# Merged second-layer weights built by GpSimd during levels 2 and 3; image 0: statistics and normalisation ahead of the output and identity products

## The chip, the core and the metric

One core of one Trainium2 chip runs the whole program. The metric is device time in microseconds (us), from start to end of one execution; lower is better. Names of engines in the rows: PE is TensorE (PEld its weight loads), DVE is VectorE, ACT is ScalarE, POOL is GpSimd, SP is SyncE, which here only issues transfers (SPq).

## What is computed

Two residual convolution layers on eight images of 64 channels, 128 by 128. Cut to what matters here:

```python
# layer 0: group norm, then four resolutions (levels 0 to 3) of conv3x3 -> relu -> conv1x1 -> attention
for i in range(LEVELS):                       # level i works at 128 / 2**i
    y = mean_pool(gn(x), 2 ** i)
    y = relu(conv3x3_dilated(y, ds_w3[i])); y = conv1x1(y, ds_w1[i])
    out += upsample(att(y))                   # 13x13 filter plus a dynamic 3x3 filter per image
x = x + conv1x1(out, fin_w)
# layer 1: a 5x5 convolution, and a 3x3 convolution seen through nine shifts weighted by wr
y3, y5 = conv3x3(gn(x)) + b3, conv5x5(gn(x)) + b5
out = einsum(stack([y5] + nine_shifts(y3)), wr) + br
x = x + out
```

In layer 1 both convolutions and the weights `wr` fold into one 5x5 convolution, the *merged weights*, plus corrections for the image borders (`row_w`, `col_w`, `cor_w`). In layer 0 the 1x1 convolutions fold into output products (`gti`, `gar`) and identity weights (`idt_h`, `idt_l`).

## The kernel before

The program is one sequence of blocks: level 1 for all eight images, then levels 2 and 3 together for four pairs of images, then level 0, then layer 1. A block ends when all engines have reached its end; the next one starts then. Every engine runs its own queue in the order of the code, and only semaphores tie the queues. Products of full precision are made as three matmuls, high by high, high by low and low by high (`product`, lines 169 to 171), so most data exist as a high and a low half, for instance `nh`, `nl` (normalised input), `rh`, `rl` (after the relu), `lk_h`, `lk_l` (large filter).

**Level 1, one image after another.** GpSimd sums 2x2 pixels of each chunk of the input (`prep_chunk`, lines 308 to 314) and VectorE takes statistics of the same chunk (line 878). VectorE combines them (line 885), TensorE averages over groups (`group_mean_pe` line 228, `group_var_pe` line 233), VectorE finishes mean and deviation and normalises in five pieces (`norm`, line 906); ScalarE makes `nh` of each piece (line 753), GpSimd `nl` (line 631). TensorE convolves five chunks of rows (`conv`), ScalarE applies the relu (lines 775, 777), VectorE makes `rh` (line 968), GpSimd `rl` (line 687). After `features` and `identity` follows `large_filter`, 28 tiles of three matmuls, of which the last six need this image's dynamic tiles from VectorE. Work for image i+1 (chunks 2 to 7, statistics, normalisation) stands between the steps of image i.

**Image 0** has extra steps. ScalarE issues all small loads before it computes anything. TensorE starts with the output products (lines 1150, 1151), VectorE copies them out (1053, 1054), TensorE makes the identity products (1155 to 1160), and only then come the group means. GpSimd clears `lks` (line 732, before `norm_low`) and SyncE then fills it and issues all other weight loads (`weights`, lines 529 to 536) before it may load chunks 2 and 3 of image 1 into `room`, for which it also waits until the identity weights have left `room` (`s_cp` of 9). GpSimd makes the low half of the large filter (`filter_low`, line 598) after chunks 5 to 7 of image 1.

**Image 7** has the merged weights. GpSimd clears four tiles (`conv5_clear`), ScalarE loads the weights into them, and after its `rl` pieces GpSimd runs `conv5_first` and nine times `conv5_shift` (lines 654 to 676), in tiles that borrow room from level 1 (`pl1`, `pln`, `xc`, `room`). ScalarE copies the result to `tile5` and `col_w` (lines 835, 837), and SyncE stores it to memory (line 592), where layer 1 reads it much later. SyncE's first wait in the next block is for that store.

**Levels 2 and 3, per pair.** GpSimd makes `rl` (line 1330), sums for the next pair, clears columns of the feature tiles (lines 1343, 1344) and makes `nl` of the next pair (line 1323). VectorE makes four sets of dynamic tiles per pair (`dynamic_tiles`, lines 191 to 206, of 768 columns; I call them tiles 1 to 4), the third in `lk_h`, `lk_l`, the others in `dt_h`, `dt_l`. TensorE runs the fixed taps, then the convolutions of the next pair with the dynamic taps in between, in the order of the four tiles. Tile 4 takes the buffer of tile 1 and waits for `dt_f`. After the last pair there are no convolutions to interleave.

## Time and profile before

| what | us |
|---|---|
| median of 3 runs | 2747.36 |
| lowest, highest | 2738.88, 2752.03 |
| the profiled execution | 2754.88 |
| its span, first to last instruction | 2753.1 |
| TensorE busy | 2481.8 (90%) |
| VectorE, ScalarE, GpSimd busy | 2094.9, 1104.4, 943.6 |
| level 1 (image 0 to the store of image 7) | 0 to about 494 |
| merged weights and their store behind it | to 511.7 |
| levels 2 and 3 | 512 to about 821 |

TensorE is busy 90% of the span, so the first question at any place is whether TensorE waits there. A row of the timeline gives start, duration, engine, line, operation, result and source, and in brackets how long the engine had been idle and what released it. "x8" means that neighbouring instructions of one line are merged. Times are from the span's start.

### The profile page before, as it was taken

The numbers are of one execution on the slowest core, as the hardware profiler recorded it, in microseconds if no ns is written. First come the engines' busy times: TensorE is split into PE (matmuls) and PEld (weight loads), VectorE is DVE, ScalarE is ACT, GpSimd is POOL, SyncE is SP. The second block draws the span as 40 slices with busy tenths as digits, with TensorE's granted clock in tenths as the row PEclk, the third lists the DMA queues.
The fourth block names the chain that finished last, engine by engine and source line by source line (L and its number), as shares of the span: only waits on it lengthen the run. The fifth ranks groups of instructions, "written<-read, shape, count | busy, mean of one in ns | idle before, by whom it ended". The sixth has DMA issues, their size and how long they took to land. (4 is left out here: it accounts for less than half of the span.)

```text
span 2753.1 us, 37560 instructions
## 1 busy us (share of the span) xinstructions
PE 2481.8 (90%) x11638; PEld 1990.3 (72%) x11638; DVE 2094.9 (76%) x2776; ACT 1104.4 (40%) x1773; POOL 943.6 (34%) x863
## 2 busy tenths in 40 slices
PE   3899999499978999999995988999849999999998
PEld 3677777388866888888884767777637777777776
DVE  5566564245548888888887898898869899998998
ACT  1332332101107898989993222222113333333331
POOL 6775666522204444444446734444010000000000
PEclk9899999788868999999997988999859999999999
DMA  7344441100008777777762134443442333333332
GB/s 137 88 113 104 102 102 42 35 14 11 10 21 199 221 219 216 222 217 213 221 192 105 65 148 150 156 156 140 166 167 67 111 114 98 96 97 110 116 99 62
DMA packets 345087, 338.82 MB, mean 123 GB/s; under 512 B 57648, under 2 KB 308400, under 8 KB 331696
## 3 DMA queue, kind: packets, MB, share of 16 engines
q1 hardware_dynamic: 337056, 335.53, 41.9%
q10 hardware_dynamic: 7952, 2.30, 0.5%
q8 instruction: 42, 0.69, 0.1%
q14 instruction: 37, 0.30, 0.0%
HBM read 211.60 MB, written 122.62 MB: 121 GB/s over the span
## 5 line engine op out<-in xcount | busy, mean ns | idle before, releaser
L169 PE MATMUL ps_all<-vh,u_h 128*128 128x512 f32 x960 | 384.6, 401 | 29.2 <-DVE vl L2945 28.4
L171 PE MATMUL ps_all<-vh,u_l 128*128 128x512 f32 x960 | 383.0, 399 | 0.0
L170 PE MATMUL ps_all<-vl,u_h 128*128 128x512 f32 x960 | 382.6, 399 | 0.0
L2854 ACT ACTIVATE vh<-rt,gn 128x528 fp32r<-128x528 f32 x192 | 131.0, 728 | 445.2 <-DVE rt L2922 319.4
L169 PE MATMUL ps_all<-vh,t_h 128*128 128x512 f32 x576 | 231.4, 402 | 23.5 <-DVE vl L1984 23.4
L1823 POOL TENSOR_TENSOR zr<-zr,z 128x256 f32<-128x256 f32 x128 | 126.5, 1008 | 336.7 <-DMA xr<-in_x 336.7
L169 PEld LDWEIGHTS ps_all<-vh,u_h 128*128 128x128 f32 x960 | 180.7, 188 | 82.8 <-issue 36.5
L170 PE MATMUL ps_all<-vl,t_h 128*128 128x512 f32 x576 | 230.2, 400 | 0.0
L171 PE MATMUL ps_all<-vh,t_l 128*128 128x512 f32 x576 | 229.4, 398 | 0.0
L171 PEld LDWEIGHTS ps_all<-vh,u_l 128*128 128x128 f32 x960 | 180.9, 188 | 46.2
L170 PEld LDWEIGHTS ps_all<-vl,u_h 128*128 128x128 f32 x960 | 181.0, 189 | 45.4
L169 PE MATMUL ps_all<-nh,w3h 128*128 128x512 f32 (+2 forms) x348 | 135.6, 390 | 45.7 <-POOL nl L1323 35.8
L1827 POOL TENSOR_TENSOR xr<-xr,zr 128x1024 f32<-128x1024 f32 x64 | 146.7, 2292 | 5.0
L169 PEld LDWEIGHTS ps_all<-vh,t_h 128*128 128x128 f32 x576 | 109.2, 189 | 50.4 <-issue 25.0
L1912 ACT ACTIVATE rp_h<-yt,b3p 128x1024 fp32r<-128x1024 f32 x64 | 142.8, 2231 | 0.0
L169 PE MATMUL ps_all<-ch,w_h 128*128 128x512 f32 x280 | 116.2, 415 | 27.0 <-POOL cl L2294 12.8
L2500 DVE TENSOR_TENSOR xq<-xq,ps_all 128x512 f32<-128x512 f32 x128 | 129.5, 1088 | 11.2 <-PE ps_all L2671 9.9
L2294 POOL TENSOR_TENSOR cl<-rw,ch 128x560 fp32r<-128x560 f32 x48 | 80.8, 1686 | 151.0 <-ACT ch L2338 151.0
L170 PE MATMUL ps_all<-nl,w3h 128*128 128x512 f32 (+2 forms) x348 | 131.5, 378 | 0.0
L171 PE MATMUL ps_all<-nh,w3l 128*128 128x512 f32 (+2 forms) x348 | 131.5, 378 | 0.0
L2945 DVE SCALAR_TENSOR_TENSOR vl<-rt,gn,vh 128x1056 fp32r<-128x1056 f32 x96 | 127.2, 1325 | 3.0 <-ACT vh L2854 3.0
L171 PEld LDWEIGHTS ps_all<-vh,t_l 128*128 128x128 f32 x576 | 108.9, 189 | 27.7
(410 smaller groups left out, 6668.4 us busy)
## 6 DMA issues: line engine op xcount, KB each, us to landing
xr<-in_x SPq DMA_DIRECT2D x128, 256.0 KB, 3.6
x_layer<-xr SPq DMA_DIRECT2D x64, 512.0 KB, 2.7
xq<-x_layer SPq DMA_DIRECT2D x32, 1024.0 KB, 4.8
x_layer<-xq SPq DMA_DIRECT2D x32, 1024.0 KB, 3.8
out<-ot SPq DMA_DIRECT2D x64, 512.0 KB, 5.1
xw<-in_x SPq DMA_DIRECT2D x112, 288.0 KB, 4.3
xw<-x_layer SPq DMA_DIRECT2D x16, 1152.0 KB, 8.6
xw<-x_layer SPq DMA_DIRECT2D x16, 1088.0 KB, 7.7
```

The lines of the kernel that those rows point to most:

```text
L169: pe.matmul(o, wh, xh, start=first, stop=False, skip_group_check=True)
L170: pe.matmul(o, wh, xl, start=False, stop=False, skip_group_check=True)
L171: return pe.matmul(o, wl, xh, start=False, stop=last, skip_group_check=True)
L1823: pool.tensor_tensor(v, v, zz, ALU.add).then_inc(z_a, 1)
L1827: pool.tensor_tensor(v, v, zz.to_broadcast([P, 512, 2]), ALU.add).then_inc(x_z, 1)
L1912: act.activation(phases(rp_h, t % 2), yt[:, :, :].rearrange("p n (q d) -> p n q d", d=4), ACT.Relu, bias=b3p[:, 0:1]).then_inc(r_h, 1)
L2294: pool.tensor_tensor(cl[:, k, :, :], src, ch[:, k, :, :].bitcast(F32), ALU.subtract).then_inc(v_l, 1)
L2500: dve.tensor_tensor(v, v, ps_all[:, 3 + dc, :].rearrange("p (n q) -> p n q", q=32), ALU.add).then_inc(qfree, 1)
L2854: act.activation(vh[:, v % 2, n, :, :].rearrange("p a b -> p (a b)"), rt[:, n, :, :].rearrange("p a b -> p (a b)"), ACT.Identity, scale=gn ...
L2945: dve.scalar_tensor_tensor(vl[:, v % 2, 2 * c:2 * c + 2, :, :].rearrange(f), rt[:, 2 * c:2 * c + 2, :, :].rearrange(f), gn1[:, bass.ds(i, ...
```

## The change

Two parts.

Merged weights: `conv5_clear`, `conv5_first` and `conv5_shift` leave image 7 of level 1 and go into the block of levels 2 and 3, with tiles of their own (`s31`, `c5`, `cls`) and with `tmp` and `wrb` in `p2` of the first images, which are used up by then. A new `merged(g)` stands at the end of GpSimd's work for pair g: clearing in pair 0, `conv5_first` and three shifts in pair 1, three shifts in pair 2, three shifts and the six copies to `col_w` in pair 3. SyncE loads the weights in pair 0 (`merged_loads`) and stores `c5` by six transfers before it stores the last pair (`merged_store`). ScalarE has no part in it. Level 1 now ends with SyncE's store of image 7.

Image 0: the table of group weights `gav` is loaded first, with a semaphore of its own. TensorE starts with the group means; the output products go behind the convolution of chunk 0, the identity products behind that of chunk 1, and they write to `ps_lk` in place of `ps_main`. VectorE does statistics and normalisation at once and copies the output products afterwards; `split_w3(1)` goes before `identity_weights`, which moves to k = 1, and so does the work on chunk 2 of image 1. On GpSimd `norm_low(0)` goes before the clearing of `lks`, and `filter_low` before chunks 5 to 7 of image 1.

```diff
@@ image 0, VectorE
-                    dve.wait_ge(s_ld, NLD)
-                    dve.wait_ge(s_mm, 1)
-                    dve.tensor_copy(gti, ps_main[0:NI, 0, 0:P].rearrange("p (a b) -> p a b", b=C)).then_inc(s_cp, 1)
-                    dve.tensor_copy(gar[:, :], ps_main[:, 0, P:P + C]).then_inc(s_cp, 1)
                     dve.wait_ge(a_p, NA_N)
                     stats_begin(0)
                     stats_end(0)
                     for k in range(NCH):
                         norm(0, k)
+                    dve.wait_ge(s_ld, NLD)
+                    dve.wait_ge(s_mm, 1)
+                    dve.tensor_copy(gti, ps_lk[0:NI, 0:P].rearrange("p (a b) -> p a b", b=C)).then_inc(s_cp, 1)
+                    dve.tensor_copy(gar[:, :], ps_lk[:, P:P + C]).then_inc(s_cp, 1)
@@ image 0, GpSimd
                     level2_sums(0)
+                    norm_low(0)
                     pool.wait_ge(bn_done, 4 + 2 * 6)
                     pool.memset(lks, 0.0).then_inc(s_zero, 1)
-                    norm_low(0)
@@ level 1, GpSimd, body
-                        if nxt:
-                            for c in range(5, NX):
-                                prep_chunk(i + 1, c)
                         if first:
                             pool.wait_ge(s_hi, 8)
                             for dr, dc in PIX:
...
                             alone(pool)
+                        if nxt:
+                            for c in range(5, NX):
+                                prep_chunk(i + 1, c)
@@ image 0, VectorE, body
                             if first and k == 0:
+                                split_w3(1)
+                            if first and k == 1:
                                 identity_weights()
-                                split_w3(1)
@@ image 0, TensorE
                         for k in range(NCH):
                             conv(i, k)
+                            if first and k == 0:
+                                output_products()
+                            if first and k == 1:
+                                identity_products()
@@ end of level 1, SyncE
-                    sp.wait_ge(t5_d, 12)
-                    sp.dma_start(cs.ap(), tile5.rearrange("p a b c -> p (a b c)")).then_inc(t5_st, 16)
+                    sp.wait_ge(l1_e, 16 * 8)
@@ levels 2 and 3, SyncE
-                    sp.wait_ge(t5_st, 16)
+                    def merged_loads():
+
+                        sp.wait_ge(w_z, 2)
+                        with nc.allow_non_contiguous_dma(reason="weights by input channel"):
+                            for r in range(2):
+                                sp.dma_start(s31[par(r), 1 - r:4 - r, :, :], c3t).then_inc(w_ld, 16)
+                                sp.dma_start(c5[par(r), 1 - r:6 - r, :, :], c5t).then_inc(w_ld, 16)
+                            sp.dma_start(wrb[:, :, :], wrt.unsqueeze(0).to_broadcast([P, 10, C])).then_inc(w_ld, 16)
+
+                    def merged_store():
+
+                        steps.at(sp, 0, NSTEP)
+                        dst = cs.ap().rearrange("p (a b c) -> p a b c", b=5, c=P)
+                        for blk in range(3):
+                            for m in range(2):
+                                sp.dma_start(dst[:, blk, :, par(m)], c5[:, 2 * blk - m + 1, :, :]).then_inc(w_st, 16)
...
+                        if g == 0:
+                            merged_loads()
+                    merged_store()
                     store(NG - 1)
                     sp.wait_ge(zst, 16 + 32 * G * NG)
+                    sp.wait_ge(w_st, 16 * 6)
@@ levels 2 and 3, GpSimd
+                    def merged(g):
+
+                        if g == 0:
+                            conv5_clear()
+                            return
+                        if g == 1:
+                            conv5_first()
+                        for sw in range(3):
+                            conv5_shift(g - 1, sw)
+                        if g == 3:
+                            assert steps.n == NSTEP, steps.n
+                            for blk in range(3):
+                                for m in range(2):
+                                    pool.tensor_copy(col_w[:, :, blk, par(m)], cls[:, :, 2 * blk - m + 1, :]).then_inc(w_c, 1)
...
                         if not last:
                             norm(g + 1)
+                            pool.wait_ge(n_l, NI1 * (g + 2))
+                            alone(pool)
+                        merged(g)
```

How the change moves instructions is shown at three places. Names are those of the tiles, with `ps_all` for all of TensorE's results; the trailing number is the shape. First, TensorE at its very start, image 0, one piece of the difference:

```order
-L1150 MATMUL ps_all<-room 48x128
-L1151 MATMUL ps_all<-room 128x64
-L1155 MATMUL ps_all<-room 128x64 x4
-L1158 MATMUL ps_all<-room 128x1 x4
-L1160 MATMUL ps_all<-room 128x1 x4
+L986 UNCONDITIONAL_BRANCH
 L228 MATMUL ps_all<-small,gav 128x1
 L233 MATMUL ps_all<-small,gav 128x1
```

The output and identity products no longer stand before the two group averages.

Second, GpSimd in image 0, from the last pieces of `rl` to the sums for level 2. Before, with three chunks of image 1 (`pl<-`) ahead of the eight filter parts (`lk_l`):

```order
L687 TENSOR_TENSOR rl<-rf,rh 128x4x64
L308 TENSOR_TENSOR pl<-xc 128x256
L311 TENSOR_TENSOR pl<-pl,xc 128x256
L314 TENSOR_TENSOR pl<-pl,xc 128x256
L308 TENSOR_TENSOR pl<-room 128x256
L311 TENSOR_TENSOR pl<-pl,room 128x256
L314 TENSOR_TENSOR pl<-pl,room 128x256
L308 TENSOR_TENSOR pl<-room 128x256
L311 TENSOR_TENSOR pl<-pl,room 128x256
L314 TENSOR_TENSOR pl<-pl,room 128x256
L598 TENSOR_TENSOR lk_l<-p,lk_h 128x28x16 x8
```

In the changed kernel, the same stretch:

```order
L622 TENSOR_TENSOR rl<-rf,rh 128x4x64
L581 TENSOR_TENSOR lk_l<-p,lk_h 128x28x16 x8
L308 TENSOR_TENSOR pl<-xc 128x256
L311 TENSOR_TENSOR pl<-pl,xc 128x256
L314 TENSOR_TENSOR pl<-pl,xc 128x256
```

The filter parts moved ahead of nine instructions.

Third, GpSimd in levels 2 and 3 at the end of pair 1, from `nl` of pair 2 to `rl` of pair 2. Before:

```order
L1323 TENSOR_TENSOR nl<-pl,nh 128x26x16 x2
L1323 TENSOR_TENSOR nl<-pl,nh 128x30x32 x2
L1330 TENSOR_TENSOR rl<-rfb,rh 128x8x16 x2
L1330 TENSOR_TENSOR rl<-rfb,rh 128x16x32 x2
L308 TENSOR_TENSOR pl<-p 128x2x128
```

In the changed kernel (`c` is the 5x5 tile, `s` the 3x3 one; `p` holds `tmp` and `wrb`):

```order
L1283 TENSOR_TENSOR nl<-pl,nh 128x30x32 x2
L1299 TENSOR_TENSOR c<-c,p 128x1920
L1304 TENSOR_TENSOR p<-s,p 128x768
L1308 TENSOR_TENSOR c<-c,p 128x4x192
L1313 TENSOR_TENSOR cls<-cls,p 128x256
L1318 TENSOR_TENSOR row_w<-row_w,p 64x192
L1321 ISA
L1321 TENSOR_SCALAR cor_w<-p 64x64
L1304 TENSOR_TENSOR p<-s,p 128x768
L1308 TENSOR_TENSOR c<-c,p 128x4x192
L1313 TENSOR_TENSOR cls<-cls,p 128x256
L1304 TENSOR_TENSOR p<-s,p 128x768
```

Fourteen computing steps of the merged weights came in between, of which the first ten are shown; pair 3 gets thirteen of them and six copies behind, and pair 2 eight, since only the first and the last three shifts touch `cls` and `cor_w`.

## Rows read from the trace of the kernel before

**Rows 1.** Busy time in stretches: PE, PEld, DVE, ACT, POOL; then granted clock, DMA, GB/s.

```profile
100.00:170.00 70.00, 69.49 (x317) 53.19 (x316) 45.33 (x79) 20.41 (x42) 41.26 (x46) 0.99 0.36 83
```

**Rows 2.** TensorE (PE), image 0, timeline: start, us, line, operation, idle before.

```profile
37.73 0.59 PE L228 MATMUL ps_all<-small,gav 128*128 128x1 f32 x2
...
44.42 0.76 PE L169 MATMUL ps_all<-nh,w3h 128*128 128x512 f32 x1 [4.82 <-POOL nl L631]
...
86.65 2.16 PE L263 MATMUL ps_all<-hdn,kg 8*128 8x1 f32 x18
96.49 0.77 PE L169 MATMUL ps_all<-fh,lk_h 128*128 128x512 f32 x1 [7.67 <-POOL lk_l L598]
```

**Rows 3.** VectorE (DVE), image 0, timeline.

```profile
25.13 1.29 DVE L878 BATCH_NORM_STATS2 stat<-xc 128x6 f32<-128x512 f32 x2 [0.32 <-DMA xc<-in_x]
...
40.51 7.48 DVE L906 TENSOR_SCALAR pln<-pl,coef 64x704 f32<-64x704 f32 x9
...
66.42 1.29 DVE L878 BATCH_NORM_STATS2 stat<-room 128x6 f32<-128x512 f32 x2 [3.00 <-DMA room<-in_x]
```

**Rows 4.** GpSimd (POOL), image 0, timeline.

```profile
32.77 3.09 POOL L732 MEMSET p<- 128x3584 f32 x1 [0.15 <-POOL room L617]
42.69 2.91 POOL L631 TENSOR_TENSOR nl<-pln,nh 128x704 fp32r<-128x704 f32 x2 [6.83 <-ACT nh L753]
46.63 2.58 POOL L631 TENSOR_TENSOR nl<-pln,nh 128x512 fp32r<-128x512 f32 x3 [1.03 <-ACT nh L753]
...
80.47 0.61 POOL L308 TENSOR_TENSOR pl<-xc 128x256 f32<-128x256 f32 x1
...
87.69 8.65 POOL L598 TENSOR_TENSOR lk_l<-p,lk_h 128x448 fp32r<-128x448 f32 x8
```

**Rows 5.** Transfers issued by SyncE (SPq), image 0, timeline.

```profile
35.89 5.21 SPq L529 DMA_DIRECT2D p<-in_lkt  x8
...
53.28 0.60 SPq L536 DMA_DIRECT2D bb<-in_br  x1
61.39 2.65 SPq L511 DMA_DIRECT2D room<-in_x  x4
```

**Rows 6.** End of level 1, timelines of SyncE and of TensorE.

```profile
491.71 2.15 SPq L559 DMA_DIRECT2D z_level<-z  x2
511.36 0.34 SPq L592 DMA_DIRECT2D conv_weights<-room  x1
...
524.63 0.58 PE L169 MATMUL ps_all<-nh,w3h 128*128 128x256 f32 x1 [35.08 <-POOL nl L1323]
```

**Rows 7.** GpSimd, 430 to 512 us, groups by shape: busy, mean ns, idle.

```profile
L659 POOL TENSOR_TENSOR room<-pl,room 128x768 f32<-128x768 f32 x9 | 16.5, 1828 | 0.7
...
L654 POOL TENSOR_TENSOR pln<-pln,room 128x1920 f32<-128x1920 f32 x1 | 4.3, 4317 | 0.0
```

**Rows 8.** VectorE beside GpSimd: timeline at 566 us; group by shape, 0 to 60 us.

```profile
566.01 2.27 DVE L196 TENSOR_TENSOR dker<-dcoef,chm 128x768 f32<-128x768 f32 x1
...
L906 DVE TENSOR_SCALAR pln<-pl,coef 64x128 f32<-64x128 f32 x1 | 1.2, 1231 | 0.0
```

**Rows 9.** Images 2 and 3 in levels 2 and 3: VectorE, then TensorE, timelines.

```profile
652.64 0.96 DVE L206 TENSOR_TENSOR lk_l<-dker,lk_h 128x768 fp32r<-128x768 f32 x1
...
664.26 0.96 DVE L206 TENSOR_TENSOR dt_l<-dker,dt_h 128x768 fp32r<-128x768 f32 x1
...
665.20 0.25 PE L169 MATMUL ps_all<-fjh,lk_h 128*128 128x128 f32 x1
...
669.56 0.25 PE L169 MATMUL ps_all<-fjh,dt_h 128*128 128x128 f32 x1
```

**Rows 10.** Images 6 and 7, the last pair: VectorE, then TensorE, timelines.

```profile
789.68 0.96 DVE L206 TENSOR_TENSOR lk_l<-dker,lk_h 128x768 fp32r<-128x768 f32 x1
...
796.56 0.32 PE L169 MATMUL ps_all<-fjh,lk_h 128*128 128x128 f32 x1
...
799.77 0.41 PE L169 MATMUL ps_all<-fjh,dt_h 128*128 128x128 f32 x1
```

More of the change, by code:

```diff
@@ L350, in conv_kernel @@
             coef = sb("coef1", [P, 2], stack=st)
[L351 removed]
+            room = sb("room", [P, 3072], stack=st)
             def part(flat, o, *shape, rows=P):
@@ L536, in weights @@
                                     sp.dma_start(bb[hp, k:k + 1], v.rearrange("(c a) -> c a", a=1)).then_inc(l1_e, 16)
-                    def weights_last():
-                        sp.wait_ge(p2_done, B)
-                        sp.wait_ge(bn_done, 4 + 2 * NX * B)
-                        with nc.allow_non_contiguous_dma(reason="small weight layouts"):
-                            sp.dma_start(wrb, wrt.unsqueeze(0).to_broadcast([P, 10, C])).then_inc(l1_lw, 16)
                     def cross(i):
@@ L632, in norm_low @@
                                                nview(nh, s0, s1_).bitcast(F32), ALU.subtract).then_inc(n_l, 1)
-                    def step(ins):
-                        steps.done(ins)
-                        steps.wait(pool)
-                    def conv5_clear():
-                        steps.start(0)
-                        pool.wait_ge(l1_e, 16 * 8)
-                        pool.wait_ge(n_l, NCH * B)
-                        pool.wait_ge(p2_done, B)
-                        pool.wait_ge(n_f, NCH * B)
-                        pool.wait_ge(bn_done, 4 + 2 * NX * B)
-                        alone(pool)
-                        pool.memset(s31, 0.0).then_inc(l1_z, 1)
-                        pool.memset(c5, 0.0).then_inc(l1_z, 1)
-                        step(pool.memset(row_w[:, :, :], 0.0))
-                        step(pool.memset(cls, 0.0))
@@ L679, in body @@
                     def body(i, nxt, nxt2, first=False):
-                        last = not nxt
                         pool.wait_ge(n_l, NCH * (i + 1))
                         alone(pool)
-                        if last:
-                            conv5_clear()
                         for k, (r0, r1) in enumerate(rows_at):
@@ L689, in body @@
                             if nxt:
-                                for c in prep_at(k):
+                                for c in prep_at(k, first):
                                     prep_chunk(i + 1, c)
-                        if last:
-                            conv5_first()
-                            for sh in range(3):
-                                for sw in range(3):
-                                    conv5_shift(sh, sw)
-                            assert steps.n == NSTEP, steps.n
-                        if nxt:
-                            for c in range(5, NX):
-                                prep_chunk(i + 1, c)
                         if first:
@@ L787, in body @@
                     def body(i, last, first=False):
-                        if last:
-                            act.wait_ge(l1_z, 2)
-                            with nc.allow_non_contiguous_dma(reason="weights by input channel"):
-                                for r in range(2):
-                                    act.dma_start(s31[par(r), 1 - r:4 - r, :, :], c3t).then_inc(l1_ld, 16)
-                                    act.dma_start(c5[par(r), 1 - r:6 - r, :, :], c5t).then_inc(l1_ld, 16)
                         if not first:
@@ L1256, in conv_kernel @@
             zst = s1("zst")
+            w_z, w_ld, w_st, w_c = s1("w_z"), s1("w_ld"), s1("w_st"), s1("w_c")
+            steps = Steps(s1("w_s"), 200)
+            NSTEP = 37
             def nview(a, lv):
@@ L1324, in norm, with step, conv5_clear @@
                                                    nview(nh, lv)[:, j].bitcast(F32), ALU.subtract).then_inc(n_l, 1)
+                    def step(ins):
+                        steps.done(ins)
+                        steps.wait(pool)
+                    def conv5_clear():
+                        steps.start(0)
+                        pool.memset(s31[:, :, :, :], 0.0).then_inc(w_z, 1)
+                        pool.memset(c5[:, :, :, :], 0.0).then_inc(w_z, 1)
+                        step(pool.memset(row_w[:, :, :], 0.0))
+                        step(pool.memset(cls[:, :, :, :], 0.0))
```

114 lines of the change are left out of this document (53 added, 61 removed).

## The prediction

> **What bounds the kernel now.** I read busy time by stretches first: from 100 us on, level 1 keeps TensorE busy 69.5 of 70 us at a granted clock of 0.99 [rows 1]. There only work of TensorE itself counts, and whatever delays or advances its large filter in image 0 is carried unchanged to the end of level 1. So the change can only matter where TensorE waits: in image 0, and between level 1 and level 2, where it is idle for 35.08 us [rows 6]. I then followed these two gaps engine by engine in the timelines, and last asked what the moved GpSimd work meets in levels 2 and 3. Level 0 and layer 1 hold the same instructions as before, and the merged weights are in memory long before layer 1, so I cost both at nothing.
>
> **Part 1, the end of level 1.** Image 7's result is stored by two transfers that SyncE issues from 491.71 to 493.86. The block does not end then, since the merged weights are still being made and stored: the last instruction is the issue at 511.36, until 511.70, and TensorE starts 12.93 us later at 524.63 [rows 6]. In the changed kernel nothing is queued behind the two transfers, so the block ends at 493.9: 511.70 - 493.86 = **17.8 us gained**. What could be late next is the landing of those two transfers, because SyncE waits for it before it exchanges halos. The halos are ready 6 us after a block starts (517.72 against 511.70, [rows 6]), so at about 499.9; the transfers have the 6 us from 493.9 too, and 1 MB in 256-byte rows takes about that. I keep 17 to 18.
>
> **Part 2, image 0.** Here several queues are moved past each other, so I go along them.
> Statistics: VectorE has the last chunk's statistics at 25.13 + 1.29 = 26.4 [rows 3]. Today the group mean stands behind the output and identity products and starts at 37.73; from there to the first normalisation it is 40.51 - 37.73 = 2.8 us [rows 2, 3]. With 0.7 for the aggregate, normalisation would start at 29.9, **10.6 us earlier**. ScalarE's small loads delay none of this: the group weights now land first.
> First convolution: GpSimd makes `nl` from 42.69 on, 2.2 us behind the first normalisation [rows 3, 4]. It is busy with sums for level 2 until 32.6, just ahead of the clearing at 32.77, and the two engines hold each other up (part 3), so I put `nl` at 33.8 and the first convolution 1.7 us behind it [rows 2, 4] at 35.5, 8.9 earlier than 44.42.
> What is late next is SyncE. The clearing of `lks` used to run at 32.77, in GpSimd's spare time, and SyncE's weight loads began when it was done, at 35.89, and kept its queue until 53.28 + 0.60 = 53.88: 18.0 us of issues [rows 4, 5]. Now the clearing stands behind the five pieces of `nl`, which take 42.69 to 49.21 = 6.5 us [rows 4]: 33.8 + 6.5 + 0.1 + 3.1 = 43.5. Then 18.0 us of issues end at 61.5. The chunks of image 1 that need `room` are behind them in the queue. Today they are issued at 61.39, held by the identity weights, and VectorE waits for them at 66.42 [rows 3, 5]. So they come at the same time as before, though for another reason. Behind them stand, in VectorE's order, the small feature weights and three pieces of `rh`, then `rl` on GpSimd, which ends at 80.5 [rows 4]. I expect that end unchanged: **almost all of the 10.6 us is lost in SyncE's queue**. The identity products now stand between convolutions on TensorE (about 5 us, of the cover of SyncE's 18), and must be through VectorE by 61.5; by my count they are at 58, with 3 us to spare.
> Large filter: it needs GpSimd's eight filter parts, 87.69 to 96.34, and starts at 96.49 [rows 2, 4]. The three chunks ahead of them take 87.69 - 80.47 = 7.2 us [rows 4]. With these behind, the parts end at 80.5 + 8.65 = 89.1. The other conditions on TensorE, the taps of this image, are done at 86.65 + 2.16 = 88.8 [rows 2], so little more could be had. **7.2 us gained**. The three chunks are needed by the normalisation of image 1, some 15 us later; they have the room. Bounds: if SyncE's loads are 2 us later than I count, 5; if they come as much earlier as the statistics do, the taps come earlier too and the sum is 7.2 + 8.9 = 16.
>
> **Part 3, the merged weights in levels 2 and 3.** The steps themselves are known: 1.83 us for each product or sum of 768 columns, 4.3 for the first one of 1920 columns [rows 7]; 13 steps of three shifts that touch the sides come to 15 us. GpSimd has this time free in each pair. The question is VectorE, which makes the four dynamic tiles just then. A VectorE operation of 768 columns takes 0.96 us alone [rows 9], and the one at 566.01 took 2.27 while GpSimd made `nl`; a normalisation of only 128 columns took 1.23 [rows 8]. The excess is what was left of GpSimd's instruction. So I take it that the two exclude each other, each instruction of one waiting for the whole one of the other; the reduction among a tile's six operations, 0.60 us, runs free. The sum is then by alternation.
> The Trainium skill, SBUF — State Buffer, section Who interferes with whom, says the same of a fast one-input or a two-input VectorE operation beside GpSimd: an exclusive lock for the whole instruction, where whoever issues first wins. If both engines merely shared bandwidth, this part would cost some 2 us; with the lock it is the sum below, so this is a rule that speaks against the change, and rows 8 agree with it.
> Pair 1: tile 3 is ready at 653.6 and read at 665.20; tile 4 at 665.2 and read at 669.56 [rows 9]. GpSimd starts its 4.3 us step at 641.2 and then alternates. VectorE's remaining work up to tile 3 (11.7 us from 641.95) waits for 3.6 us of the first step and ten further steps of 13.3 us, less 3 that run beside the reductions: tile 3 at 667.7, 2.5 late. Tile 4 needs 4.9 + 1.0 more, 673.5, against 665.20 + 2.5 + 4.36 = 672.1: 1.4 late. **4 us lost**. Pair 2 has eight steps, about 10 us of delay, inside the 11.6 us that tile 3 has to spare: nothing.
> Pair 3: no convolution is interleaved, so tiles are read sooner. Tile 3 is ready at 790.6 and read at 796.56 [rows 10]; thirteen steps, less what runs beside, push it by about 11 to 801.7. Tile 4 follows 4.9 us later at 806.6, where TensorE took it at 799.77 [rows 10]: **7 us lost**, passed on to the end of the block. Bounds for both pairs together: 2 (the waits are hidden) and 16 (the gaps let TensorE run on at half speed for a few us more).
>
> **Sum.** -17.8 - 7.2 + 4 + 7 = -14.0 us. On the profiled execution of 2754.88 that is 2740.9; the median of the runs is 7.5 below that one, so 14 off the median gives **2733.4**. A measurement of this kernel can tell about 0.5%, 13.7 us, from no change: my forecast lies on that line.
>
> **Rivals.**
> A, the sum as it stands (from -10 to -18): chance 0.45, 2733.4.
> B, VectorE's tiles are not late enough to stop TensorE, for instance because short steps let it pass: -17.8 - 7.2 + 2 = -23, so 2724. For it: tile 4 of pair 1 misses by only 1.4 in my count. Against: in pair 3 all slack is 6 and the delay 11. Chance 0.2.
> C, SyncE's queue does not hold image 0 back, and the early statistics count in full: -17.8 - 16 + 11 = -23, also 2724. Against it stand the 18.0 us of issues. Chance 0.08.
> D, image 0 gains less, because the later weight loads hold it (-5), or the gaps in levels 2 and 3 cost 16: -17.8 - 5 + 16 = -7, so 2740. Chance 0.23.
> E, slower: TensorE's speed in levels 2 and 3 depends on gaps. Its products of 128 columns take 0.25 us each in pair 1 [rows 9] and 0.41 in the last pair [rows 10], behind the busy stretch. If the new gaps make it run at the lower of its clocks through pairs 1 to 3, each us of its work there costs one more. It turns slower than before from 14 us of such work, and 28 us of it give 2761. For the gaps I count (4 and 7 us) this is far. Chance 0.04.
> That the change does not do what it says, for instance that the block still ends late because the store of image 7 holds the halos, would give back up to 6 of the 17.8: it is in D.
>
> **How the numbers follow.** A is likeliest: 2733.4. B and C end at 2724, and 2721 with the better ends of parts 1 and 2; D ends at 2741. I take **2721 to 2742**, which leaves out E and the tails of the others. Faster by over 0.5% (below 2733.6): half of A, and B and C, 0.52. Within 0.5%: the other half of A and D, 0.45. Slower: 0.03.
>
> **What would show it.** Right: the last transfer of level 1 issued near 486.7 and TensorE's first product of level 3 some 13 us behind it; first normalisation near 30, SyncE's load of `room` still near 61, large filter at 89.3; VectorE operations of 1.5 to 2.8 us in the tiles of pairs 1 and 3, and TensorE waiting for them 2 to 6 us. Wrong: loads of `room` at 56 or earlier (C), no wait of TensorE for VectorE in levels 2 and 3 (B), a granted clock below 0.7 through pairs 1 and 2 (E).

## The result, and where it came from

The changed kernel takes 2728.13 us (median of 20 runs), the one before 2747.74 (20 runs): 19.6 us less, a ratio of 0.9935 with a 95% interval of 0.9923 to 0.9947, so 15 to 21 us. The profiled execution spans 2726.3 us against the 2753.1 of the kernel before. That is 26.8 us, of which 18.6 are followed below. The rest stands where both kernels hold the same instructions: level 0 is 3.8 us shorter; in levels 2 and 3, with pairs counted from 0, 2.5 are gained around the end of pair 0 and 2.6 around the end of pair 2, and 0.9 are lost at the start of pair 2; level 1 gains another 0.3 behind image 0. At the ends of these two pairs the same products of 512 columns take 0.39 us now and 0.63 before: TensorE's clock stood at different levels in the two executions.

**Image 0.** TensorE's timeline in the changed kernel, to be read against [rows 2]: group mean, first convolution, first product of the large filter.

```profile
27.49 0.56 PE L228 MATMUL ps_all<-small,gav 128*128 128x1 f32 x2 [27.49 <-DVE small L802]
...
34.93 0.77 PE L169 MATMUL ps_all<-nh,w3h 128*128 128x512 f32 x1 [5.60 <-POOL nl L614]
...
89.83 0.48 PE L169 MATMUL ps_all<-fh,lk_h 128*128 128x512 f32 x1 [0.55 <-POOL lk_l L581]
```

The mean starts at 27.49 instead of 37.73 and the convolution at 34.93 instead of 44.42, but at the large filter the gain is 6.7 us: 89.83 against 96.49. VectorE [rows 3] has the first normalisation at 30.25, the end of the identity weights at 58.11, and then 9.27 us idle for a chunk of image 1:

```profile
30.25 8.74 DVE L823 TENSOR_SCALAR pln<-pl,coef 64x704 f32<-64x704 f32 x9
...
58.11 0.29 DVE L857 TENSOR_TENSOR idt_l<-room,idt_h 128x128 fp32r<-128x128 f32 x1
67.68 1.29 DVE L795 BATCH_NORM_STATS2 stat<-room 128x6 f32<-128x512 f32 x2 [9.27 <-DMA room<-in_x]
```

GpSimd [rows 4]: `nl`, the clearing of `lks` behind it, the last `rl`, and the filter parts right behind that:

```profile
33.23 1.55 POOL L614 TENSOR_TENSOR nl<-pln,nh 128x704 fp32r<-128x704 f32 x1 [0.18 <-ACT nh L682]
...
40.63 3.09 POOL L662 MEMSET p<- 128x3584 f32 x1
...
79.27 1.68 POOL L622 TENSOR_TENSOR rl<-rf,rh 128x384 fp32r<-128x384 f32 x2
80.90 8.79 POOL L581 TENSOR_TENSOR lk_l<-p,lk_h 128x448 fp32r<-128x448 f32 x8
```

SyncE's queue [rows 5]: the weights that wait for the clearing, the last small load, the load of `room`:

```profile
43.76 5.22 SPq L521 DMA_DIRECT2D p<-in_lkt  x8
...
61.99 0.60 SPq L528 DMA_DIRECT2D bb<-in_br  x1
62.70 2.65 SPq L503 DMA_DIRECT2D room<-in_x  x4
```

The load of `room` is issued 0.1 us after the last small load is through. The last `rl` ends at 80.95, 0.4 us later than before: nothing is left there of the 10 us. The 6.7 us come from the filter parts alone, which start right behind it, at 80.90 instead of 87.69, since the three chunks no longer stand between.

**The boundary.** SyncE's last store of level 1 and the first halos of the next block, then TensorE's first product there [rows 6]:

```profile
484.76 2.20 SPq L544 DMA_DIRECT2D z_level<-z  x2
493.24 0.51 SPq L1225 DMA_DIRECT2D pl<-pl  x1
...
500.20 0.58 PE L169 MATMUL ps_all<-nh,w3h 128*128 128x256 f32 x1 [17.55 <-POOL nl L1283]
```

From store to halos it is 8.48 us where it was 26.01, and TensorE waits 17.55 us where it waited 35.08. That is 17.5.

**Levels 2 and 3.** From the first halos to the first instruction of the next block (VectorE's MEMSET at 821.66 before, at 798.58 now) it was 821.66 - 517.72 = 303.9 us and is 798.58 - 493.24 = 305.3. In the last pair, the end of tile 2 (`dt_h`, `dt_l`) and of tile 3 (`lk_l`) on VectorE, and TensorE's two waits for tiles there [rows 10]:

```profile
761.45 2.09 DVE L204 CAST dt_h<-dker 128x768 fp32r<-128x768 f32 x1
763.57 2.48 DVE L206 TENSOR_TENSOR dt_l<-dker,dt_h 128x768 fp32r<-128x768 f32 x1
...
770.75 0.96 DVE L206 TENSOR_TENSOR lk_l<-dker,lk_h 128x768 fp32r<-128x768 f32 x1
...
771.76 0.48 PE L169 MATMUL ps_all<-fjh,lk_h 128*128 128x128 f32 x1 [1.91 <-DVE lk_l L206]
...
776.61 0.48 PE L169 MATMUL ps_all<-fjh,dt_h 128*128 128x128 f32 x1 [0.75 <-DVE dt_l L206]
```

GpSimd's steps beside the first two of these lines:

```profile
760.67 2.44 POOL L1304 TENSOR_TENSOR p<-s,p 128x768 f32<-128x768 f32 x1
763.20 2.04 POOL L1308 TENSOR_TENSOR c<-c,p 128x768 f32<-128x768 f32 x1
```

The CAST of 761.45 stands 2.09 us and ends 0.43 after GpSimd's first step; the TENSOR_TENSOR of 763.57 ends 0.81 after the second, at 766.05 against 765.24, and takes 2.48 where it takes 0.96 alone. VectorE waits for most of what is left of GpSimd's instruction and then finishes its own. Following both pairs row by row on TensorE, pair 1 lost 1.8 us: unchanged products run 26.95 us earlier than before ahead of its two waits for tiles (0.66 and 0.64 us) and 25.14 earlier behind them. Pair 3 lost 3.8: 2.7 are the two waits shown, and the rest is that the products on tile 3 take 0.41 us each from the first on, where the first ones took 0.29 to 0.36 before. The sum is -17.5 - 6.7 + 5.6 = -18.6, against 19.6 at the medians.

### The profile page after: what moved, and what is told of

Same layout as the page of the kernel before. It is cut to its first block and busy times, and to the rows that moved or that the text cites. A ratio compares the mean times of both kernels' runs of the same rounds, so it can differ in the third digit from the quotient of the medians.

```text
span 2726.3 us, 37560 instructions
## 1 busy us (share of the span) xinstructions
PE 2472.6 (91%) x11638; PEld 1982.3 (73%) x11638; DVE 2122.3 (78%) x2776; ACT 1100.0 (40%) x1761; POOL 964.5 (35%) x869
```

## Experiments

All ratios are against the kernel before, run on the same chip beside the variant. "The stretch" is the time from the first halos to the end of the block of levels 2 and 3, in the profiled execution.

| kernel | median us | runs | ratio (95%) | large filter, image 0 | last store, level 1 | stretch |
|---|---|---|---|---|---|---|
| before | 2747.74 | 20 | 1 | 96.49 | 491.71 | 303.9 |
| after | 2728.13 | 20 | 0.9935 (0.9923-0.9947) | 89.83 | 484.76 | 305.3 |
| image0_only | 2740.08 | 12 | 0.9969 (0.9959-0.9979) | 91.02 | 486.65 | 300.8 |
| merged_only | 2734.05 | 6 | 0.9947 (0.9934-0.9961) | 96.41 | 491.81 | 311.3 |
| early_clear | 2732.72 | 6 | 0.9939 (0.9921-0.9957) | 89.58 | 484.62 | 311.5 |
| no_steps | 2722.08 | 6 | 0.9906 (0.9886-0.9925) | 90.16 | 486.07 | 302.4 |
| late_small | 2727.94 | 6 | 0.9934 (0.9910-0.9959) | 86.30 | 481.95 | 305.3 |
| pairs012 | 2728.46 | 7 | 0.9939 (0.9918-0.9960) | 90.76 | 484.87 | 304.5 |
| memset_steps | 2727.57 | 6 | 0.9932 (0.9906-0.9958) | 89.82 | 484.69 | 303.7 |
| gaps | 2724.74 | 6 | 0.9920 (0.9896-0.9944) | 89.70 | 485.65 | 303.8 |
| best | 2720.47 | 5 | 0.9918 (0.9901-0.9935) | 86.92 | 482.56 | 301.2 |
| after_again | 2721.86 | 5 | 0.9921 (0.9905-0.9937) | 90.19 | 485.16 | 304.9 |
| double_steps | 2740.70 | 12 | 0.9977 (0.9959-0.9995) | 89.40 | 485.31 | 320.0 |
| late_stats | 2719.73 | 5 | 0.9879 (0.9856-0.9901) | 78.93 | 476.42 | 302.5 |

The intervals are 5 to 14 us wide, so for the large filter and the last store the columns tell more than the medians. The stretch is less sure than it looks: image0_only and the kernel before hold the same instructions there and take 300.8 and 303.9 us, and gaps, best and late_stats, again alike there, take 303.8, 301.2 and 302.5. A difference of up to 3 us in this column cannot be put down to an edit by itself; what decides is which waits for tiles a trace has.

**The two parts apart: image0_only and merged_only.** image0_only is the kernel before with the orders of image 0 changed; merged_only is the changed kernel with them as before.

> The kernel before with only image 0's part of the change (statistics and normalisation ahead of the output and identity products, filter_low ahead of chunks 5 to 7, lks cleared after nl); the merged weights stay at the end of level 1. If the parts add up as in the prediction: level 1's end (the store of the last image) about 7 us earlier than before, the boundary of 33 us between the blocks unchanged, the time about 7 us less than before (2734 to 2744 expected, 2740 as the centre). If the gain of the whole change came from the boundary alone (rival: image 0 is worth nothing), the time is that of before and the large filter of image 0 starts at 96.5 us.

> The changed kernel with image 0 put back as it was before (products first, clearing of lks ahead of nl, chunks 5 to 7 ahead of filter_low); the merged weights are made in levels 2 and 3. Theory: the boundary gives 17.5 us back and pairs 1 and 3 take about 5, so about 12.5 us less than before (2735 as the centre). By the prediction's own terms (11 us lost in pairs 1 and 3) it is 7 us less (2741). Together with the run of image 0 alone, the two gains should add up to the 19.6 us of the whole change within 3 us; if they do not, the parts interact.

Measured at the medians: 7.6 and 13.6 us less, together 21.2, against 19.6 for the whole. The boundary in merged_only is 500.28 - 491.81 = 8.5 us, as in the changed kernel, and image 0's large filter moves by 5.5 in image0_only. As far as these intervals tell, the parts are independent. The 7 us that the prediction's own terms give for merged_only lie outside its interval (11 to 18 us). The rival that image 0 is worth nothing is out.

**What holds image 0: early_clear.**

```diff
-                    norm_low(0)
                     pool.wait_ge(bn_done, 4 + 2 * 6)
                     pool.memset(lks, 0.0).then_inc(s_zero, 1)
+                    norm_low(0)
```

> The changed kernel with one move undone: lks is cleared ahead of nl of image 0 again. Theory (SyncE's queue is held by the weight loads that wait for the clearing, and the loads of room stand behind them): the weight loads start 7 to 8 us earlier (about 36 us), the loads of room about 4 us earlier (58 to 59 us instead of 62.7), VectorE's chunk 2 of image 1 with them, and the large filter of image 0 starts at 85 to 86 us instead of 89.8; the time falls by about 4 us against the changed kernel, 24 against the one before. nl of image 0 comes up to 3 us later, which costs 0 if VectorE's wait for room ends last. Rival (the queue is not what ends last): the loads of room go out at 62 us as before, the later nl costs 2 to 3 us, and the time is 2 to 3 us above the changed kernel.

The theory is wrong, and the rival is right that the load goes out at 62 as before, though not in the time, which cannot be told from that of the changed kernel (0.9939 against 0.9935). SyncE's queue is free at 54.50 and yet `room` is loaded only at 62.39; the rows below say why (SyncE, GpSimd, VectorE):

```profile
53.90 0.60 SPq L528 DMA_DIRECT2D bb<-in_br  x1
62.39 2.65 SPq L503 DMA_DIRECT2D room<-in_x  x4
...
33.32 3.15 POOL L661 MEMSET p<- 128x3584 f32 x1 [0.15 <-POOL room L600]
36.55 2.94 POOL L614 TENSOR_TENSOR nl<-pln,nh 128x704 fp32r<-128x704 f32 x2
...
30.32 11.57 DVE L823 TENSOR_SCALAR pln<-pl,coef 64x704 f32<-64x704 f32 x9
45.70 0.28 DVE L976 COPY room<-ps_all 48x128 f32<-48x128 f32 x1 [3.82 <-PE ps_all L1034]
...
62.07 0.29 DVE L857 TENSOR_TENSOR idt_l<-room,idt_h 128x128 fp32r<-128x128 f32 x1
```

The load also waits for the identity weights, which end at 62.36 here and at 58.40 in the changed kernel. `nl` now stands behind the clearing and starts at 36.55 instead of 33.23; TensorE's first convolution waits for it and starts at 38.30 instead of 34.93, and with it the output and identity products and what VectorE makes of them come 3 to 4 us later. VectorE's normalisation beside the clearing is slower too, 11.57 us instead of 8.74, but VectorE then idles 3.82 us for TensorE, so this is not what ends last. The queue and the identity weights change places as the wait that ends last, and the large filter stays where it is (89.58). The prediction named the queue and missed that undoing the cause would not give the time back.

**The queue alone: late_small.** The small loads of `wrs` and `bb` leave the function `weights` and go behind the first turn:

```diff
                     turn(0, True, True)
+                    small_weights()
                     with sp.Fori(1, B - 2) as i:
```

> The changed kernel with the eight small loads of wrs and bb (56.76 to 62.59 us in SyncE's queue) put behind SyncE's turn of image 0, so that the loads of room stand right behind the weights of the kernel generator. Theory (in the changed kernel the queue ends last, and next behind it the identity weights, done at 58.4 us, for which the same loads wait): the loads of room go out at 58.4 instead of 62.70 us, chunk 2 of image 1 on VectorE at 63.4 instead of 67.68, the large filter of image 0 starts at about 85.6 instead of 89.83, and the time falls by 4.2 us against the changed kernel. Rival (another wait takes over: the loads of chunks 4 to 7, or the weights of the first layer): the room loads go out early but the large filter starts less than 2 us earlier, no change of the time.

SyncE's last weight load and the load of `room` behind it, and TensorE's large filter:

```profile
50.61 5.78 SPq L523 DMA_DIRECT2D kg<-in_kgw  x8
58.11 3.77 SPq L503 DMA_DIRECT2D room<-in_x  x4
...
86.30 0.48 PE L169 MATMUL ps_all<-fh,lk_h 128*128 128x512 f32 x1
```

Now the identity weights (58.08) release the load; it goes out 4.6 us earlier, the large filter starts 3.5 us earlier, and level 1 ends 2.8 us earlier. The queue was what ended last, and it ended 4.2 us behind the next condition. The time does not show the 3 us (ratio 0.9934 against 0.9935).

**Are the steps what costs in levels 2 and 3: no_steps.** GpSimd's multiplications and additions are left out, so the merged weights come out unmultiplied.

```diff
                         if g == 1:
-                            conv5_first()
-                        for sw in range(3):
-                            conv5_shift(g - 1, sw)
+                            pool.wait_ge(w_ld, 16 * 5)
```

> The changed kernel without the merged weights' arithmetic: GpSimd's multiply and add steps of pairs 1 to 3 are left out (the clearings, the loads, the store and the six copies stay; the merged weights come out as unmultiplied). Theory by the two traces: 5 us less than the changed kernel, 1 to 1.5 of it in pair 1 and about 4 in pair 3, VectorE's tiles of pair 3 done at 0.96 us per 128x768 TENSOR_TENSOR where the changed kernel has 2.1 to 2.5. By the prediction's terms it is 11 us less; by the rival that the waits are hidden it is 0.

TensorE no longer waits for `lk_l` or `dt_l` (4.0 us in the changed kernel), and the stretch is 302.4 us, 2.9 less than in the changed kernel's profile, which is within the spread named above. The ratio says 0.9906 against 0.9935, 8 us, with intervals that touch. The waits come from the steps; that they are hidden is out by the rows, and the size in time is open between 3 and 8 us.

**Is it what GpSimd reads: memset_steps.** The same steps as MEMSETs of 1.7 and 0.7 us (the merged weights come out as zeros):

```diff
-                        step(pool.tensor_tensor(d, d, tmp[:, :, :, :], ALU.add))
+                        step(pool.memset(c5[:, :, :, :], 0.0))
```

> The changed kernel with every multiply and add step of the merged weights replaced by MEMSETs of a like length (c5 whole for 1.7 us, cls whole for 1.0 us; some 20 us in pair 1 instead of 26.7), so GpSimd is as busy but reads nothing; the merged weights come out as zeros. Theory (VectorE and GpSimd exclude each other on SBUF whatever GpSimd does): VectorE's 128x768 TENSOR_TENSORs beside them take 1.7 to 2.6 us instead of 0.96 and TensorE waits for lk_l in pair 3 as in the changed kernel; time within 2 us of the changed one. Rival (only GpSimd's instructions that read two inputs hold VectorE): VectorE's at 0.96 us throughout, the waits gone, and a time like that without the steps, 6 to 8 us less than the changed kernel.

Two MEMSETs of GpSimd in pair 1, and VectorE beside them:

```profile
619.77 1.70 POOL L1303 MEMSET c<- 128x1920 f32 x1
621.53 2.00 POOL L1304 MEMSET c<- 128x1920 f32 x1
```

```profile
620.61 1.27 DVE L204 CAST dt_h<-dker 128x768 fp32r<-128x768 f32 x1
621.92 0.96 DVE L206 TENSOR_TENSOR dt_l<-dker,dt_h 128x768 fp32r<-128x768 f32 x1
```

The TENSOR_TENSOR from two buffers runs its 0.96 us beside a MEMSET; the CAST, 0.56 alone, takes 1.27 and ends 0.41 after the MEMSET of 619.77. So it depends on both sides. The waits for the tiles are gone and the stretch is 303.7. The ratio (0.9932) is not that of no_steps, though the intervals overlap, so the rival is right on the mechanism and unproven on the time. Nor is the time a clean comparison: the MEMSETs of pair 1 are through at 635.0, the steps of the changed kernel at 641.0. The Trainium skill, SBUF — State Buffer, section Who interferes with whom, states just this division: an operation with two SBUF inputs contends with a GpSimd instruction that reads SBUF, not with one that only writes. The trace agrees (0.96 us); the prediction had used the rule in a coarser form, which was enough for steps that all read.

**Where the steps stand: pairs012 and gaps.** pairs012 makes them in pairs 0 to 2:

```diff
-                        if g == 1:
+                        if g == 0:
                             conv5_first()
                         for sw in range(3):
-                            conv5_shift(g - 1, sw)
+                            conv5_shift(g, sw)
```

> The changed kernel with the merged weights' steps one pair earlier (pairs 0, 1, 2 instead of 1, 2, 3; the clearings ahead of pair 0, the ten shift weights loaded behind the halos of pair 1). Pair 3, where TensorE has no convolution of a next pair to run beside VectorE's tiles, is left alone. Theory: pair 3's two waits of TensorE for VectorE (1.9 and 0.75 us) and the 3.8 us that pair 3 lost go; pair 0 now loses what pair 1 lost (1 to 2 us): 2 to 3 us less than the changed kernel. Rival (any late tile costs, whatever stands beside it): the loss moves from pair 3 to pair 0, no change.

The waits of pair 3 are gone. One wait of 0.79 us for `lk_l` and one of 0.64 for `dt_l` are left, at the end of pair 0's tiles. The stretch is 0.8 us shorter, which is within the spread named above; the ratios are alike. gaps keeps pairs 1 to 3, but does the steps where GpSimd waits for something else:

```diff
                         for k, (lv, j) in enumerate(items):
+                            if k == 3:
+                                merged(g, 0)
...
                             sums3(g + 1)
+                        merged(g, 1)
                         pool.wait_ge(qfree, 2 + Q * g + 4)
```

> The changed kernel with the same steps at other places of pairs 1 to 3: GpSimd does them in its two waits of 10 to 13 us (ahead of the last rl of the pair, and ahead of the edge clearings of fjh and fjl) instead of behind nl, where VectorE makes the tiles of the dynamic filters. Theory: VectorE's tiles go back to 0.96 us an instruction, TensorE's waits for lk_l and dt_l go, and the time is 5 to 8 us below the changed kernel, that of the kernel without the steps. Rival: VectorE's eight additions of the attention and its fl (0.9 us for four of them, TensorE waits behind them for the buffer) are held instead, TensorE waits 0.5 to 1 us more at each of eight additions in pairs 1 to 3, and the time is that of the changed kernel or some us above it.

The tiles are back at 0.96 us an instruction, but for the two that stand beside `nl` as in the kernel before (2.27 and 2.55 in pair 1), and TensorE waits for none. What VectorE does there instead is its normalisation, from one buffer, here in the timeline of gaps:

```profile
594.91 2.70 DVE L1485 TENSOR_SCALAR pl<-pl,stat 128x128 f32<-128x128 f32 x2
597.53 4.12 DVE L1485 TENSOR_SCALAR pl<-p,stat 128x512 f32<-128x512 f32 x2
```

In the changed kernel these two lines take 0.60 and 1.00 us. They are held for 5.2 us in pair 1, and nobody waits for it. The additions of the attention, which read PSUM, take 0.92 us beside GpSimd's steps as without them; so the rival's delay does not exist. The stretch is 303.8 us; by the ratios the time is 4 us below that of the changed kernel, less than the 5 to 8 expected and inside the interval.

**Twice the steps: double_steps.**

```diff
+                        step(pool.tensor_tensor(tmp[:, :, :, :].rearrange("p a b c -> p (a b) c"),
+                                               s31[:, :, :, :].rearrange("p a b c -> p (a b) c"),
+                                               wrb[:, shift_tap(sh, sw), :].unsqueeze(1).to_broadcast([P, 12, C]), ALU.mult))
                         step(pool.tensor_tensor(tmp[:, :, :, :].rearrange("p a b c -> p (a b) c"),
```

> The changed kernel with each of the nine multiplications of the shifts done twice (GpSimd busy some 6 us longer in each of pairs 1 to 3, same result). Theory (VectorE gets about one instruction in for each of GpSimd's two-input steps, and loses about 1.3 us to each step that stands beside its tiles): three more steps beside the tiles delay lk_l by 3 to 5 us in pairs 1 and 3; TensorE's wait for it grows from 1.9 to 5 to 6 us in pair 3 and to 4 to 7 us in pair 1, and the time is 6 to 12 us above the changed kernel. Rival (the steps' cost is not the delay of the tiles): the waits stay as they are and so does the time.

TensorE's two longest waits for `lk_l`, in pairs 1 and 3:

```profile
642.48 0.47 PE L169 MATMUL ps_all<-fjh,lk_h 128*128 128x128 f32 x1 [2.18 <-DVE lk_l L206]
...
786.97 0.47 PE L169 MATMUL ps_all<-fjh,lk_h 128*128 128x128 f32 x1 [5.41 <-DVE lk_l L206]
```

Pair 3 is as expected (5.4), pair 1 is not (2.2): from the first instruction of its tiles to `lk_l` VectorE takes 31.9 us where it takes 30.5 in the changed kernel, so the added multiplications cost it 1.4 us there and not 3 to 5. Why so little was not followed. All waits for tiles add up to 9.9 us where the changed kernel has 4.0, yet the stretch is 14.7 us longer and the median of the runs 18.8 above that of the changed kernel run beside it (15 by the ratios). Of these 14.7 us, 1.5 are lost in pair 0, ahead of any step; some 7 are more than the waits. In the 24 us from 644 and from 668 us the granted clock is 0.71 and 0.54 where the changed kernel has 0.79 and 0.71.

**One execution against the other: after_again.**

> The changed kernel itself, on the same chip as its variants. By what the variants show, TensorE's wait for lk_l in pair 1 is either 0.6 to 0.8 us (then the stretch from the first halos to the end of the block for levels 2 and 3 takes about 305 us) or about 2 us (then about 311 us, with the granted clock below 0.73 in the 24 us that follow). One of the two is expected, nothing between.

It had the short wait (0.84 us), and a stretch of 304.9. The long one was seen in other kernels whose levels 2 and 3 are the same, as in the pair below. Changed kernel: GpSimd and VectorE, and below them busy time by stretches from 644 and from 668 us (TensorE busy, then granted clock, DMA, GB/s).

```profile
633.04 2.63 POOL L1304 TENSOR_TENSOR p<-s,p 128x768 f32<-128x768 f32 x1
...
633.05 0.96 DVE L196 TENSOR_TENSOR dker<-dcoef,chm 128x768 f32<-128x768 f32 x1
```

```profile
644.00:668.00 24.00, 22.32 (x159) 0.79 0.11 25
668.00:692.00 24.00, 23.01 (x112) 0.71 0.06 14
```

early_clear, whose levels 2 and 3 hold the same instructions, with TensorE's wait, and the same stretches:

```profile
633.04 1.82 POOL L1304 TENSOR_TENSOR p<-s,p 128x768 f32<-128x768 f32 x1
...
633.05 2.63 DVE L196 TENSOR_TENSOR dker<-dcoef,chm 128x768 f32<-128x768 f32 x1
635.71 2.46 DVE L200 TENSOR_TENSOR dker<-dker,lk_base 128x768 f32<-128x768 f32 x1
...
640.30 0.47 PE L169 MATMUL ps_all<-fjh,lk_h 128*128 128x128 f32 x1 [2.00 <-DVE lk_l L206]
```

```profile
644.00:668.00 24.00, 23.53 (x142) 0.71 0.02 6
668.00:692.00 24.00, 22.26 (x126) 0.65 0.14 33
```

GpSimd's step and VectorE's TENSOR_TENSOR are issued within 0.01 us. In the first GpSimd's step is the one that was held (2.63 us), in the second VectorE's. There the tile is 1.25 us later, TensorE waits 2.00 us instead of 0.66, and then has a granted clock of 0.71 and 0.65 instead of 0.79 and 0.71; the stretch is 311.5 us instead of 305.3. merged_only shows the second kind too (2.06 us, 311.3). In all three executions with a wait of 2 us there (double_steps is the third) the granted clock behind it was lower. The rows show it from the first product behind the wait: those of 128 columns take 0.41 us where the changed kernel's take 0.29, and those of 512 take 0.63 where they take 0.43. That the wait is the cause is likely by this order, but stays open: no run changed the one without the other. Whether one program shows both kinds is not shown either: each variant has one profile, and the two of the changed kernel both have the short wait. The six runs of early_clear speak for it: three lie at 2725.7 to 2729.8 us and three, the profiled one among them, at 2735.6 to 2738.0.

**Both moves, and a third: best and late_stats.** best is late_small and gaps together.

> Both moves together: the eight small loads behind SyncE's turn of image 0, and the merged weights' steps in GpSimd's two waits of pairs 1 to 3. Theory (the two are independent, in different blocks): level 1's end 3 us earlier than in the changed kernel (the last store of level 1 at about 482), no wait of TensorE for lk_l or dt_l, and the stretch from the first halos to the end of the block for levels 2 and 3 at 301 to 304 us; 5 to 8 us below the changed kernel run beside it. Rival: with the stretch at the mercy of the granted clock, nothing beyond 2 us can be told from the changed kernel.

Both moves show in its trace (last store 482.56, stretch 301.2 with no wait for a tile), 6.2 us earlier at the end of the block than in after_again, 792.29 against 798.49. The medians, 2720.47 and 2721.86, do not tell them apart, so for the time the rival holds. What TensorE still waits for in image 0 of best:

```profile
72.73 0.55 PE L169 MATMUL ps_all<-rh,fa_h 128*128 128x256 f32 x1 [11.11 <-POOL rl L627]
...
86.92 0.48 PE L169 MATMUL ps_all<-fh,lk_h 128*128 128x512 f32 x1 [0.27 <-POOL lk_l L586]
```

11.11 us for an `rl` that stands, on GpSimd and VectorE, behind two chunks of image 1 that are still being loaded. late_stats is best with these chunks moved behind the last `rl`:

```diff
-                return [(), (2, 3), (4,), (), ()][k] if first else [(2,), (3,), (4,), (), ()][k]
+                return [(), (), (), (), (2, 3)][k] if first else [(2,), (3,), (4,), (), ()][k]
...
-                            for c in range(5, NX):
+                            for c in range(4 if first else 5, NX):
...
+                        if first:
+                            prep_chunk(i + 1, 4)
```

> The two moves of the kernel best, and a third for image 0: its rl and rh pieces go ahead of image 1's chunks 2, 3 and 4 on GpSimd and VectorE (chunks 2 and 3 behind the last piece, chunk 4 behind filter_low on GpSimd), since TensorE waits 11.1 us there for an rl that stands behind two chunks still on their way. Theory (those chunks, not the rl itself, are what TensorE waits for): that wait falls under 2 us, the large filter of image 0 starts near 78 to 80 us instead of 86.9, the block's last store near 475 instead of 482.6, and the time is 6 to 8 us below the kernel best. Rival (image 1's statistics are then too late): TensorE waits that long at image 1's first convolution instead (0.75 us now, its nl is done 8.6 us before it), and the time stays as it is.

```profile
62.74 0.36 PE L169 MATMUL ps_all<-rh,fa_h 128*128 128x256 f32 x1 [1.94 <-DMA kg<-in_kgw]
...
78.93 0.48 PE L169 MATMUL ps_all<-fh,lk_h 128*128 128x512 f32 x1 [1.74 <-POOL lk_l L586]
...
105.17 0.48 PE L169 MATMUL ps_all<-nh,w3h 128*128 128x512 f32 x1 [1.44 <-DVE ga_l L884]
```

The wait is 1.94 us (a new one of 2.51 us follows, for a sum that VectorE now makes behind the two chunks), the large filter starts 8.0 us earlier than in best, the last store 6.1 earlier, and image 1's convolution still waits only 1.44. Against the kernel before the ratio is 0.9879, 31 us less at the medians and 33 by the ratio: faster than the changed kernel too, whose intervals begin at 0.9923 and 0.9905 in its two measurements, above the 0.9901 where this one ends.

## Why the prediction was right, and where it was not

- **Time.** Forecast 2733.4 in 2721 to 2742; measured 2728.1. It lies between rivals A (2733.4) and B (2724), and what happened has a part of each. The terms as measured add up to -18.6. That this meets the 19.6 of the medians within 1 us is partly luck, since stretches of the same instructions differ by 2.5 to 3.8 us between the two profiled executions.
- **Part 1, 17.8.** Measured 17.5. The halos start 6.28 us behind the last issue, where they started 6.02 behind the block's end before, so the landing of the last store costs 0.3 us at most. Right.
- **Part 2, 7.2.** Measured 6.7 (image0_only: 5.5), and for the reason given: the filter parts ahead of the chunks, with the 10 us of the early statistics lost in SyncE's queue. The steps hold one by one: normalisation 30.25 (forecast 29.9), `nl` 33.23 (33.8), convolution 34.93 (35.5), clearing done 43.7 (43.5), identity weights 58.4 (58). The queue ended at 62.6 instead of 61.5. TensorE's identity products took 2.8 us, not 5, which mattered to nobody. late_small shows that the queue did hold `room`, as the prediction said against rival C. What it left out is that the early clearing is no cure (early_clear): it delays `nl`, and by it the identity weights, by what it saves SyncE.
- **Part 3, +11: the term that was mis-sized.** Measured 1.8 in pair 1 (forecast 4) and 3.8 in pair 3 (forecast 7), 5.6 together. The mechanism stands, and so do the waits of TensorE and their places; pair 2 has none, as forecast. The step that failed is the alternation, in which every step of GpSimd was charged in full to VectorE. In pair 3 tile 3 was 7.9 us late and not 11: that is the sum of what VectorE's instructions up to `lk_l` took above their time alone, since each paid only for the rest of a step already under way. The other part fell on GpSimd, whose thirteen steps took 20.8 us there from first to last instead of 15.8. In pair 1 tile 3 was done at 639.0; unchanged work just ahead of it runs 26.9 us earlier than before, so that is 665.9 on the clock of the kernel before, where 667.7 was forecast and TensorE reads it at 665.2 [rows 9]: 0.7 late instead of 2.5.
- **Rival E** (a lower clock through the gaps) was given 0.04 and made to wait for 14 us of work. Something like it is seen on a smaller scale, beyond the waits themselves: some 5 us in early_clear and merged_only, 7 in double_steps, with the cause likely and not shown. The prediction had put it in the range as part of D only ("16: the gaps let TensorE run on at half speed").

## What to carry to other kernels

When work is moved into an engine's idle time, ask which instructions of its neighbour stand beside it, and choose the idle time whose neighbours read PSUM or have slack; the same steps made TensorE wait 4.0 us in one gap of the pair and not at all in another. When a wait has two conditions, work out the second before moving the first: here the queue and the identity weights were 4 us apart, and the obvious repair made the one 8 us earlier and the other 4 us later, which only swapped them. The largest gain left was found by asking what stood ahead of the awaited instruction in its engine's own order, not what that instruction itself needed.

## What the runs showed of the hardware

- GpSimd and VectorE: a VectorE TENSOR_TENSOR with both inputs in SBUF is held by a GpSimd TENSOR_TENSOR (0.96 us alone, up to 2.63 beside it) and not by a MEMSET (0.96); a CAST and a TENSOR_SCALAR are held by a MEMSET too (CAST 0.56 alone, 1.27 beside it; the normalisation of image 0 takes 8.74 us, and 11.57 beside a clearing of 3.15). A TENSOR_REDUCE (0.60) is held by neither, and additions that read PSUM (0.92) are not held by GpSimd's TENSOR_TENSORs.
- Where GpSimd's and VectorE's instructions start within 0.01 us, either of the two can be the one held: GpSimd's in the changed kernel (2.63 us), VectorE's in early_clear (2.63), with the same instructions in that block, and levels 2 and 3 differ by 6 us.
- Eight loads of a weight or a bias column cost SyncE's queue 5.8 us (0.6 us each, one 1.4); with them out of the way the chunk behind was loaded 4.6 us earlier.
